# Filling unit 0's stacks from the split pieces in SBUF, and spreading the late projections over the first max rows

## The reference, cut to what matters

```python
x.shape == (2, 1024, 128)                       # 16 heads of width 8
qkv = x @ qkv_w.T + qkv_b
q, k, v = split(qkv)                            # per head
scores = einsum('bhid,bhjd->bhij', q, k) / sqrt(8) - dist[i, j] * slope[h]
attn = softmax(scores, axis=-1)
out = einsum('bhij,bhjd->bhid', attn, v)
```

## Time and profile before

| what | value |
|---|---|
| median of 3 runs | 644.01 us |
| the runs | 641.0 to 646.68 us |
| the profiled execution's own time | 648.19 us |
| its span | 645.9 us |
| PE busy | 535.9 us, 83% of the span |
| DVE, ACT, POOL busy | 400.7, 343.4, 207.1 us |

### The profile page before, as it was taken

One profiled execution on the slowest core, in us unless ns is written; L12 is line 12 of the kernel. 1 busy time (PEld: TensorE's weight loads), 2 busy tenths in 40 slices (PEclk: granted clock), 3 DMA queues, 4 the chain that ended last, 5 costly groups with the idle time before them and its releaser, 6 DMA issues.

```text
span 645.9 us, 11458 instructions
## 1 busy us (share of the span) xinstructions
PE 535.9 (83%) x4355; PEld 289.0 (45%) x4355; DVE 400.7 (62%) x658; ACT 343.4 (53%) x668; POOL 207.1 (32%) x381
## 2 busy tenths in 40 slices
PE   5589999999999999999999989998822307999920
PEld 4324444444454545444544444453312305888720
DVE  2598787787986586988677798863064311222217
ACT  5127676676677676757777666865602101323304
POOL 4255614101143151047023124510406140445440
PEclk9588999999999999999999999997856556999975
DMA  8522342223222222222111222100000002434124
GB/s 175 157 87 73 75 118 80 78 89 113 77 86 91 76 93 77 76 71 68 55 39 52 85 62 67 53 2 21 14 16 33 1 17 63 128 92 128 47 68 145
DMA packets 47125, 47.60 MB, mean 74 GB/s; under 512 B 12864, under 2 KB 36834, under 8 KB 47073
## 3 DMA queue, kind: packets, MB, share of 16 engines
q1 hardware_dynamic: 40145, 33.26, 18.2%
q0 software_dynamic: 5312, 12.34, 6.0%
q10 hardware_dynamic: 1616, 1.31, 0.6%
HBM read 31.87 MB, written 16.06 MB: 74 GB/s over the span
## 4 chain that ended last, share of the span: by engine, by line
PE 73%; DVE 15%; DMA 4%; issue 3%; ACT 2%; POOL 1%; another core or an unknown queue 1%; SPq 0%; ACTq 0%; POOLq 0%; DVEq 0%
PE ps L764 32%; PE ps L802 17%; DVE row_max L1176 7%; PE ps L931 6%; PE ps L943 5%; PE ps L767 4%; PE ps L710 1%; PE ps L828 1%; DVE heads L1228 1%; DVE x_tok L1381 1%; DMA k_stacks<-k_dram 1%; PE ps L846 1%; PE ps L816 1%; PE ps L920 1%; POOL xd L653 1%
## 5 line engine op out<-in xcount | busy, mean ns | idle before, releaser
L1176 DVE TENSOR_REDUCE row_max<-ps 128x1 f32<-128x1024 f32 x256 | 297.3, 1212 | 86.3 <-PE ps L764 43.5
L1023 ACT ACTIVATE probs<-ps 128x512 f32<-128x512 f32 x512 | 268.1, 607 | 94.7 <-PE ps L767 54.2
L764 PE MATMUL ps<-k_stacks,q_stacks 96*128 96x512 bf16 x512 | 166.0, 391 | 12.1 <-DVE row_max L1176 5.6
L764 PE MATMUL ps<-q_stacks,k_stacks 99*128 99x512 bf16 x512 | 164.5, 384 | 4.1 <-ACT probs L1023 2.7
L802 PE MATMUL ps<-probs,v_unit 128*32 128x256 f32 x2048 | 126.7, 389 | 0.0
L767 PE MATMUL ps<-distance,slope_eye 128*128 128x128 bf16 x512 | 113.8, 222 | 0.0
L802 PEld LDWEIGHTS ps<-probs,v_unit 128*32 128x32 f32 x2048 | 61.0, 111 | 55.5 <-issue 12.2
L764 PEld LDWEIGHTS ps<-k_stacks,q_stacks 96*128 96x128 bf16 x512 | 44.0, 99 | 93.1 <-DVE row_max L1176 34.2
L764 PEld LDWEIGHTS ps<-q_stacks,k_stacks 99*128 99x128 bf16 x512 | 49.0, 98 | 57.6 <-ACT probs L1023 20.0
L767 PEld LDWEIGHTS ps<-distance,slope_eye 128*128 128x128 bf16 x512 | 50.5, 99 | 26.7 <-issue 3.4
L1091 ACT ACTIVATE probs<-ps 128x640 f32<-128x640 f32 x32 | 22.4, 703 | 69.8 <-PE ps L931 69.1
(11 more groups left out here) (181 smaller groups left out, 407.5 us busy)
## 6 DMA issues: line engine op xcount, KB each, us to landing
k_stacks<-k_dram SPq DMA_DIRECT2D x63, 144.0 KB
q_stacks<-q_dram SPq DMA_DIRECT2D x63, 72.0 KB
k_stacks<-in_c_alibi_k SPq DMA_DIRECT2D x32, 96.0 KB
w<-in_w SPq DMA_DIRECT2D x12, 256.0 KB
xd<-blank POOLq DMA_DIRECT2D x8, 325.0 KB, 2.7
probs<-xd SPq DMA_DIRECT2D x8, 325.0 KB
out_dram<-out_t SPq DMA_DIRECT2D x16, 128.0 KB
yt<-zeros POOLq DMA_DIRECT2D x4, 512.0 KB, 3.0
```

Of the source, the lines that this page charges most:

```text
L764: mm = pe.matmul(out, lhs, rhs, start=True, stop=not on_diagonal)
L1023: act.activation(probs[:, k % KEPT, HALF * e:HALF * (e + 1)], ps[:, n % RING, :], ACT.Exp).then_inc(ring_read, 1)
L1176: dve.tensor_reduce(row_max[:, m % 2, i:i + 1], max_pair(k).rearrange("p a n -> p (a n)"), AX.X, ALU.max).then_inc(mx_used, 1)
```

## The change

1. **Unit 0's stacks come straight from `parts`.** Each piece 0, 1 and 2 gives 3 copies for each head, of 24 rows of 1 KB (8 partitions of the source, each to 3 rows): POOL issues the 9 copies of the first head (`first_loaded`), SP the 9 of the second (`loaded_direct`), each piece's as soon as its `q3_ready` has come. PE waits for the first head's copies at row 0 and for the second's at row 4. The two DRAM loads of each head go.
2. **The saves move from SP to ACT**, behind the second cast of piece 2. So do the two copies of turned tokens (`x_kept[2]`, `x_kept[3]`), which were DVE's.
3. **Piece 3 becomes a late piece** (FIRST = 3): ACT projects it behind the saves, POOL splits it and saves it. The tile and PSUM bank stay. Pieces 4 to 7 follow one step later on POOL: piece 4 between `split_max(0)` and `split_max(1)`, pieces 5, 6, 7 in the loop in units 0, 1, 2 (before: 6 and 7 in units 0 and 1).
4. **Late projections after rows 3, 5, 7 and 9**, the transposes after row 11.

```diff
-FIRST = 4
+FIRST = 3
...
+        def first_copies(y, e):
+
+            c, half = piece(y)[1:]
+            rows = slice(DH * head_of(0, e), DH * head_of(0, e) + DH)
+            for i in range(PARTS):
+                to = slice(PARTS * DH * i, PARTS * DH * (i + 1))
+                if c == 0:
+                    yield (q_stacks[to, 0, HALF * e:HALF * (e + 1)],
+                           parts[rows, y, i, :].unsqueeze(1).broadcast_to([DH, PARTS, HALF]))
+                else:
+                    yield k_stacks[to, 0, e, HALF * half:HALF * (half + 1)], parts[rows, y, :, :]
...
+            def first_stack(y):
+
+                sp.wait_ge(q3_ready, y + 1)
+                for out, src in first_copies(y, 1):
+                    sp.dma_start(out, src).then_inc(loaded_direct, 16)
...
             for y in range(3):
-                save(y)
+                first_stack(y)
             for b in range(3):
                 sp.wait_ge(parts_saved[b], SAVED[b])
-            load_parts(0, (0,))
             load_parts(1)
-            save(3)
             load_parts(2)
             load_max(0)
...
-            for b in range(3):
-                pool.wait_ge(parts_saved[b], SAVED[b])
-            h = head_of(0, 1)
-            pool.dma_start(k_stacks[0:PRODUCTS, 0, 1, :], k_dram[0, h].rearrange("d p n -> (d p) n").unsqueeze(
-                0).broadcast_to([PARTS, PARTS * DH, N])).then_inc(first_loaded, 16)
-            pool.dma_start(q_stacks[0:PRODUCTS, 0, HALF:N], q_dram[0, h, :, :, 0:HALF].rearrange(
-                "p d n -> (p d) n").unsqueeze(1).broadcast_to([PARTS * DH, PARTS, HALF])).then_inc(first_loaded, 16)
+            for y in range(3):
+                pool.wait_ge(q3_ready, y + 1)
+                for out, src in first_copies(y, 0):
+                    pool.dma_start(out, src).then_inc(first_loaded, 16)
...
-                if m < 2:
-                    split_rest(6 + m)
+                if m < 3:
+                    split_rest(5 + m)
...
-                if i in (1, 2, 3, 4):
-                    y = FIRST + i - 1
+                if i in (3, 5, 7, 9):
+                    y = 4 + (i - 3) // 2
...
-                if i == 5:
+                if i == 11:
...
             act.wait_ge(bq_ready, 1)
-            for y in range(FIRST):
-                project(y)
-                if y >= 1:
-                    second_part(y - 1)
-            second_part(FIRST - 1)
-            for y in range(FIRST, 8):
+            project(0)
+            project(1)
+            second_part(0)
+            project(2)
+            second_part(1)
+            second_part(2)
+            for g in range(2, 4):
+                act.wait_ge(x_turned, g + 1)
+                act.copy(x_t[:, g * 512:(g + 1) * 512], ps[:, TURN_BANK[g], :]).then_inc(x_kept[g], 1)
+            save(0)
+            save(1)
+            save(2)
+            project(3)
+            act.wait_ge(loaded_direct, 16 * 3 * PARTS)
+            act.wait_ge(first_loaded, 16 * 3 * PARTS)
+            for y in range(4, 8):
                 project(y)
...
-            for y in range(3):
+            for y in range(FIRST):
                 second_left(y)
                 if y >= 1:
                     third_part(y - 1)
-            third_part(2)
-            keep_turned(2)
+            third_part(FIRST - 1)
             dve.wait_ge(ld_bias, 16)
-            keep_v(0)
-            keep_turned(3)
-            second_left(3)
-            keep_v(1)
-            third_part(3)
-            keep_v(2)
-            keep_v(3)
+            for g in range(4):
+                keep_v(g)
```

61 lines of the change are left out of this document (34 added, 27 removed).

## The result

The changed kernel takes 640.84 us (median of 20 runs, 637.74 to 646.3) where the kernel before, on the same chip and in turn with it, takes 644.72 us (20 runs, 641.0 to 647.77). The ratio is 0.9954, 95% interval 0.9934 to 0.9975: 0.46% faster, 3.0 us, half of what was forecast. The ratio is not the quotient of the two medians, which would be 0.9940, or 3.9 us. The mean of the three ratios is 0.9971, a gain of 1.9 us (by the medians 3.9, 2.2 and 1.6, on the mean 2.6). The change is faster, by less than the 1% that one measurement tells apart.

The account below looks back on a forecast made before the run. Opening: a DRAM trip ahead of row 0, then DVE-bound rows; the loop is PE-bound, so opening gains arrive one for one. 5.2 + 0 + 0.8 = 6.0 us off the median 644.01 gives 638.0 us, range 634.5 to 642.0.

Parts of the forecast that it names:

- Row 0 comes earlier: Opening: earlier split of piece 2 and no DRAM trip start row 0 at 21.4, gain 5.2 us (3.5 to 5.8).
- The earlier split of piece 2: Opening: without piece 3's projection ahead of ACT's second cast, DVE's last subtraction ends at 15.75, 1.3 us earlier.
- the landing: Before row 0: a copy on POOL's queue takes 2.9 us from issue to landing, bounds 2.3 and 4.6.
- What might hold the next rows: Rows 1, 4 and 8: no wait expected; unit 1's stacks land by 29.3, row 8 near 34, covered by 4.7 us.
- a sign of being wrong: Row 8: the prediction said it is wrong if this row waits for a stack.
- The rival in which ACT's issues hide the gain: Opening: ACT's five issues cost over 1.1 us each, holding piece 3 and row 1; 643 us, chance 0.07.
- The moved splits on POOL: Loop: piece 7 moves from unit 1 to unit 2, about 5 us of POOL; priced at nothing, 1 us without cover.
- Rows 0 to 15: Row 0 to loop: DVE stalls 1.4 to 2.6 us against 2.05 before, so zero gain, bounds 0.6 either way.
- A wait before row 4: Rows before the loop: row 4's scores end 1.4 us late for DVE while PE's clock is low.
- The one I had for row 6: Rows before the loop: row 6's scores end up to 1.2 us late for DVE.
- The clock at the loop's start: Loop's first rows: shorter thin stretch of PE half restores the clock, gain 0.8 us (1.6 gain to 0.7 loss).
- The rival in which the clock holds: Row 15 and loop's start: clock stays up, gain 7.4 us in all, 636.6 us, chance 0.23.

Follow-up runs that it names:

- saves_behind_copies: Changed kernel with ACT projecting piece 3 and waiting for the first head's copies to land before issuing its five saves: 642.2 us, ratio 0.9979 to the kernel before.
- copies_only: Changed kernel with the late projections put back after rows 1 to 4 and the transposes after row 5: 640.84 us, ratio 0.9955 to the kernel before.
- spread_only: Kernel before with only its late projections moved after rows 3, 5, 7, 9 and the transposes after row 11: 641.42 us, ratio 0.9977.
- warm rows: Changed kernel with one unused 256-column matmul on PE after each of rows 11 to 15: 642.0 us, ratio 0.9932 to the kernel before.
- warm_gap_rows_again: Repeat: changed kernel plus eight unused 256-column matmuls before row 0 and one after each of rows 11 to 15: 638.4 us, ratio 0.9925 to the kernel before.
- after_again: Changed kernel measured a second time, unaltered: 643.86 us against 646.09 for the kernel before, ratio 0.9983.
- after_third: Changed kernel measured a third time, unaltered, in one batch with warm kernels: 641.36 us, ratio 0.9975 to the kernel before.
- warm gap and rows: Changed kernel plus eight unused 256-column matmuls before row 0 and one after each of rows 11 to 15: first measured 638.45 us, ratio 0.991 to the kernel before.

## Why the prediction came out as it did

It said 638.0 us, a gain of 6.0; measured was 3.0 in the first comparison and 1.9 as the mean of three. The range of 634.5 to 642.0 holds the time, but the forecast had the gain at twice what it was. In the profiled pair the opening is 2.9 us shorter where 6.0 were summed: 1.1 us are missing from row 0's term, 1.7 from the clock's (+0.8 forecast, -0.88 measured from the swap to the first values, the maxima's trip included), and 0.3 from the rows'. Point by point:

**Row 0 comes earlier: the mechanism right, the term mis-sized.** The forecast was 5.2 us; it was 4.06 from mark to mark, 3.6 over three traces. POOL was read rightly: nine copies back to back at 0.56 us where I took 0.61, from the end of the weight copy on (at 13.95 and not 13.44, since that copy took 0.82 us here against 0.31), the last issued at 18.51 where I had 18.32. The earlier split of piece 2 came as worked out: DVE's third parts of pieces 1 and 2 stand in one run (14.84 to 16.30), not with 1.40 us of waiting between. What failed is the landing: **2.9 us taken, 4.3 measured** (issue at 18.51, landing at 22.86, row 0 at 23.10), within my bounds (2.3 to 4.6) and near the worse. I had taken it between two transfers of POOL's queue that ran when the DMA engines had little else to do, and wrote beside it that the copies run beside 1.15 MB of saves without pricing that. The nearest row was the right kind of transfer in the wrong company: saves_behind_copies has 2.14 us with the saves away.

**What might hold the next rows: failed for row 8.** I had the last save of K landing at 21.3 and unit 1's loads at 29.3, covered by 4.7 us, and so priced this wait at nothing. They came at 24.56 and 35.51, and row 8 waited 1.12 us (0.24 and 1.17 in the other two traces), which the prediction had named as a sign of being wrong. Three steps of the sum were wrong: 0.57 us for each of ACT's issues, read from saves of Q with 128 rows, where each of the two K saves has 384 rows and took 0.93 and 2.63 us; 2.8 us for the save's landing, 6.42 measured; 5.55 for K's load, 8.42 measured. The first two were durations from a kernel whose saves were issued one after the other as the pieces came. The third was the wrong row: unit 0's K load, while unit 1's own took 8.09 us in the same trace. It took both errors to hold row 8: with the load issued at 23.7 as forecast and 8.42 us for it, or issued at 27.09 with 5.55, the stacks would have landed at 32.1 or 32.6, ahead of row 8's turn near 34.4. The rival in which ACT's issues hide the gain has a slip of its own: five issues at 1.8 us put row 1 at 3.6 us late, not 3.2; its condition didn't come. Piece 3 on ACT came at 20.87, not 19.8, early enough for row 1. The moved splits on POOL cost nothing, as said: DVE's waits in unit 3's rows are 1.39 and 1.45 us, before 1.40 and 1.45.

**Rows 0 to 15: the number right, in part by luck.** 21.4 +- 0.7 was forecast from row 0 to the loop's first matmul, and 22.07 measured, 20.43 and 21.06 in the other two traces, one of them outside. A wait before row 4 of 1.4 us was worked out, and 1.44 is there in the trace. The one I had for row 6 (up to 1.2) is not there; row 8's, of 1.12, which no term of the sum had, stands in its place. That the spreading buys nothing holds on top of the copies (copies_only); that it buys nothing of itself is not shown (spread_only).

**The clock at the loop's start: failed.** I took half of it as restored, a gain of 0.8 us. The thin stretch did get shorter, and the clock fell all the same, in each of the three traces of the changed kernel, at 44.0 to 44.7, and was back at 47.8 to 51.6. From the swap to the first values are 17.00, 15.19 and 16.07 us against 16.12 before: a gain of nothing on the mean, a loss of 0.88 in the profiled pair. The rival in which the clock holds was priced at 1.6 us of gain. The kernels with warm rows show more: 13.8 us in all four, 2.3 less than before, and with the eight matmuls ahead of row 0 besides, warm_gap_rows_again measured 3.2 us faster than the changed kernel beside it, with intervals that do not meet. The Trainium skill, page "TensorE: Matmul & The Clock Gate", section "What's actually happening", says that activity releases the throttle, and that the moment varies between runs. The traces agree with both: five small matmuls kept the clock up, and the changed kernel's clock rose 3.8 us earlier in one execution than in another. The Trainium skill, same section, gives half a microsecond for the variation; what was measured here is far more.

**Not foreseen at all:** the trip of unit 0's maxima through DRAM. Before, it was over before the loop needed it; with row 0 earlier and the trip at 2.60 + 2.32 us (before 1.47 + 2.66), PE waited 1.22 us in the profiled execution. About 0.7 of that is the trip's, the rest DVE's, since PE begins 0.15 us behind the freeing of the bank where the trip is over (44.36, row at 45.17); in after_again and after_third the trip cost under 0.2. It varies, and no experiment here tied it to a cause.

**What stays open.** The three openings of the changed kernel are 2.9, 4.8 and 4.0 us shorter than the one of before, on the mean 3.9, while the measured gain is 1.9 us on the mean (2.6 by the medians). Of before there is one trace. From the first to the last matmul on the values the 17 traces take 405.2 to 410.0 us, and what lies behind that 175.7 to 180.1, whatever the opening; either spreads by more than the difference, and I can't place it. Also open is why ACT's second K save takes 6.42 us to land, how much of that is the copies and how much its own neighbours, and what spreading would bring where row 8 is not held.

**The version to take** is the changed kernel with warm gap and rows: 0.991 and 0.9925 in two batches.

## What to carry to other kernels

A transfer's time from issue to landing, and the time its engine takes to issue it, belong to the company it had: before carrying such a row to a changed order, add up the bytes that will be in flight in the same microseconds, and when these exceed what the row had beside it, take the worse bound. And take the row of the transfer itself where the old trace has one: unit 1's K load was there with 8.09 us, and the 5.55 of another load was used for it. When the wait for a trip through DRAM is taken away at one place, look at once for the next load that makes the same trip, since it will have less cover by exactly what was gained. Where the stretch just ahead of a PE-bound loop leaves PE half idle, a few unused matmuls in those gaps can be worth as much as the change itself: here five of them took 2.3 us off the way from the swap to the first values, in four traces of four. In time that was 3.3 us by the ratios and 1.9 by the medians, with overlapping intervals, where the change itself brought 1.9 and 2.6.

## What the runs showed of the hardware

- A copy of 24 KB within SBUF, 8 partitions each spread to 3 rows, costs POOL 0.54 to 0.61 us to issue, in every trace, and lands 2.1 us later when no save is beside it, 3.1 to 3.6 (median of the six K copies), up to 5.3, beside 1.15 MB of saves.
- The same copies on SP's queue took 7.44 us for six beside the saves, 1.24 each, and 4.21, 0.70 each, without them. On ACT's queue the second K save took 2.63 us to issue beside the copies, and 0.65 behind them. That issuing waits until earlier transfers drain is a reading of this and was not tested; on POOL's queue the issues kept their length though the landings grew.
- One load of 144 KB of K from DRAM, spread to 72 rows, took 5.8 us with the slopes and piece 3's save out of the way, 7.1 to 7.4 beside the slopes, 8.1 to 9.0 beside both, 9.8 to 10.0 with half of the saves besides.
- The granted clock fell at 44.7 behind a stretch in which PE was busy 0.67 of the time (the window at 43 us) and stayed at 1.00 where the same stretch was busy at 0.97. At 0.50, 1.2 GHz, the maxima of the loop's first rows start 2.02 us apart (46.33 and 48.35) and DVE waits for PE; at 1.00, 2.4 GHz, eight follow each other in 9.10 us.
